# Expert tiles of 256 rows of one expert become tiles of two 128-row halves with an expert each

## What is computed

```
def _ffn(xf, w1, b1, w2, b2):
    h = jnp.maximum(xf @ w1 + b1, 0.0)
    return h @ w2 + b2
logits = x_flat @ router_w + expert_bias
top_vals, top_idx = jax.lax.top_k(logits, TOP_K)          # TOP_K = 2, 16 experts
weights = jax.nn.softmax(top_vals, axis=-1)
...
for e in range(N_EXPERTS):
    y_e = _ffn(x_flat, routed_w1[e], routed_b1[e], routed_w2[e], routed_b2[e])
    routed_out = routed_out + comb[:, e:e + 1] * y_e       # comb is 0 for experts not chosen
return shared_out + routed_out
```

## Time and profile before

| | |
|---|---|
| time, median of 3 runs | 887.23 us (885.23 to 887.95) |
| span of the profiled execution | 888.7 us |
| TensorE (PE) busy | 794.8 us, 89% |
| VectorE (DVE) busy | 471.0 us, 53% |
| ScalarE (ACT) busy | 483.6 us, 54% |
| GpSimd (POOL) busy | 552.2 us, 62% |
| mean DMA rate | 71 GB/s |

### The profile page before, as it was taken

The page is one execution under the profiler, slowest core; times in us unless marked ns, Lnnn a source line. Parts: engine busy times, 40 slices in busy tenths (PEclk is TensorE's granted clock), DMA queues, the critical chain, the costliest instruction groups (busy, mean ns, idle before and its releaser), DMA issues.

```text
span 888.7 us, 24132 instructions
## 1 busy us (share of the span) xinstructions
PE 794.8 (89%) x8070; PEld 572.5 (64%) x8071; DVE 471.0 (53%) x1381; ACT 483.6 (54%) x1147; POOL 552.2 (62%) x691
## 2 busy tenths in 40 slices
PE   4788999999999999999977679999999999999791
PEld 1344556655566565655554359999999999988440
DVE  2436787677767877678754423333333333332076
ACT  2355666566556666565644316666666665655147
POOL 5445588787878888787876624555555555445344
PEclk9988999999999999999999879999999999999997
DMA  5001021220222112220115321222222222221394
GB/s 165 13 27 27 19 61 56 68 62 25 61 58 65 46 40 62 62 62 29 48 32 186 124 71 46 70 70 67 71 65 65 65 65 61 65 64 46 109 317 142
DMA packets 70324, 63.44 MB, mean 71 GB/s; under 512 B 8002, under 2 KB 61640, under 8 KB 70112
## 3 DMA queue, kind: packets, MB, share of 16 engines
q1 hardware_dynamic: 60816, 44.99, 18.0%
q0 software_dynamic: 9152, 17.07, 5.9%
q10 hardware_dynamic: 272, 0.26, 0.1%
HBM read 38.75 MB, written 25.50 MB: 72 GB/s over the span
## 4 chain that ended last, share of the span: by engine, by line
PE 72%; issue 7%; POOL 6%; DVE 6%; ACT 3%; another core or an unknown queue 2%; DMA 2%; DVEq 0%; SPq 0%; POOLq 0%; ACTq 0%
PE psO L616 16%; PE psB L605 15%; PE psO L541 7%; PE psP L332 5%; PE psB L485 4%; POOL w_ring L945 3%; PE psO L548 3%; PE psB L443 3%; PE psP L407 2%; PE psP L323 2%; PE psB L475 2%; PE psP L596 2%; PE psP L347 2%; PE psB L463 2%
## 5 line engine op out<-in xcount | busy, mean ns | idle before, releaser
L988 POOL DMA_INDIRECT expert_results<-yw_all,rows x158 | 155.3, 983 | 160.0 <-ACT yw_all L863 131.2
L616 PEld LDWEIGHTS psO<-w_sb,hide 128*128 128x128 f32 x1264 | 152.9, 192 | 6.6 <-issue 2.9
L616 PE MATMUL psO<-w_sb,hide 128*128 x1264 | 154.6, 275 | 0.6 <-ACT hide L855 0.5
L965 POOL DMA_INDIRECT dispatched_rows<-rows,slot x128 | 131.0, 1023 | 36.7 <-issue 32.6
L855 ACT ACTIVATE hide<-psB,w_ring 128x256 f32<-128x256 f32 x316 | 123.6, 474 | 54.6 <-PE psB L605 50.8
L605 PE MATMUL psB<-x1T,w_ring 128*128 128x256 f32 x632 | 149.9, 380 | 0.7 <-DVE x1T L1289 0.4
L1302 DVE TENSOR_TENSOR K<-psO,b_sb 128x256 f32<-128x256 f32 x79 | 33.6, 425 | 173.0 <-PE psO L616 141.8
L605 PEld LDWEIGHTS psB<-x1T,w_ring 128*128 128x128 f32 x632 | 113.9, 190 | 13.9 <-issue 1.7
L945 POOL TENSOR_TENSOR w_ring<-w_ring,tot 128x128 f32<-128x128 f32 (+2 forms) x160 | 117.9, 758 | 0.0
L863 ACT ACTIVATE yw_all<-K,rows 128x128 f32<-128x128 f32 x158 | 54.8, 394 | 79.3 <-issue 48.4
L1040 DVE SCALAR_TENSOR_TENSOR psP<-psP,cols,delta 128x512 f32<-128x512 f32 x80 | 57.4, 754 | 71.7 <-PE psP L332 71.7
(11 more groups left out here) (174 smaller groups left out, 1311.5 us busy)
## 6 DMA issues: line engine op xcount, KB each, us to landing
rows<-dispatched_rows SPq DMA_DIRECT2D x80, 132.0 KB
w_sb<-expert_results SPq DMA_DIRECT2D x8, 1024.0 KB, 11.9
h_res<-in_hidden SPq DMA_DIRECT2D x16, 256.0 KB
out<-w_sb SPq DMA_DIRECT2D x16, 256.0 KB, 2.3
hT<-in_hidden_t SPq DMA_DIRECT2D x15, 256.0 KB, 4.6
w_sb<-in_w SPq DMA_DIRECT2D x14, 256.0 KB
expert_results<-yw_all,rows POOLq DMA_INDIRECT x158
dispatched_rows<-pad_rows SPq DMA_DIRECT2D x17, 132.0 KB
```

Of the source, the lines that this page charges most:

```text
L616: last = mm(psO[:, p, s * 128:(s + 1) * 128], hide[p][:, c, s * 128:(s + 1) * 128], w2_sb[:, bass.ds(e, 1), c, :].rearrange("p e c -> p (e ...
L965: G.indirect_dma_start(rows_dram[:, :], bass.IndirectOffsetOnAxis(slot[u % 2][:, j, k:k + 1], 0), rows[k][u % 2][:, j, :], None).then_inc( ...
L988: G.indirect_dma_start(back_dram[:, :], bass.IndirectOffsetOnAxis(row_in[i][:, s, AT_DEST:AT_DEST + 1].bitcast(u32), 0), yw[i][:, s, :], N ...
```

## The change

A tile is still 256 rows, but now two halves of 128 (`PART`), and the table gives each half its own expert and its own first row. Counts are rounded up to 128: (16384 + 16 x 127) / 128, rounded down, is 143 halves, so 72 tiles in place of 79. The buffers of rows and results go from 8 to 6 (`RING`), those of w1 from 4 tiles to 3 (`W_RING`), each now of two copies. `load_rows` issues one DMA of 128 rows for each half, four for a pair of tiles. `e_up` makes eight products of 128 columns in place of four of 256, half by half. `e_w1` copies w1 twice and also copies b2 of both experts into a new buffer, `b2b`. A new VectorE operation, `e_hid2`, does the two half-tile activations of hidden block 2; ScalarE does the other six, and waits for VectorE's before block 3. TensorE reads two registers per tile in `e_down`. VectorE's loop is now `e_y(j)`, `e_xT(j + 3)`, `e_w1(j + 3)`, `e_hid2(j + 2)`. `make_table` makes twice as many entries, and the pads are half as long.

```diff
 ST = 256
 SUB = ST // 128
-RING = 8
-W_RING = 4
-ETILES = (N * TOPK + EXPERTS * (ST - 1)) // ST
-TABLE = -(-ETILES // RING) * RING
-CAP = N + ST
+RING = 6
+W_RING = 3
+PART = 128
+ETILES = -(-((N * TOPK + EXPERTS * (PART - 1)) // PART) // SUB)
+TABLE = -(-ETILES // RING) * RING * SUB
+CAP = N + PART
...
+        w1b = [[w1_ring[:, 2 * i + s, :] for s in range(SUB)] for i in range(2)]
+        w1b.append([t[:, 0:HIDDEN + HC] for t in (o_sq[:, :, :].rearrange("p n v -> p (n v)"), R_near[:, :, :, :].rearrange("p c h t -> p (c h t)"))])
+        b2b = [mixed[i // 2][:, i % 2, :].rearrange("p (s c) -> p s c", c=C) for i in range(W_RING)]
...
-            def load_rows(j, i):
+            def load_rows(j, i, turn):
                 if not (isinstance(j, int) and j < RING):
-                    sp.wait_ge(sem(f"e_back{i // 2}"), (j - i) * (2 * SUB * 16 // RING))
+                    sp.wait_ge(sem(f"e_back{i // 2}"), turn * (2 * SUB * 16))
                 for t in range(2):
-                    sp.nop(nofuse=True)
-                    r = sp.value_load(tile_ri[0:1, bass.ds(j + t, 1)], min_val=0, max_val=EXPERTS * CAP)
-                    sp.dma_start(row_in[i + t], rows_dram[bass.ds(r, ST), :].rearrange("(s p) c -> p s c", p=128)).then_inc(sem(f"e_rows_in{i // 2}"), 16)
+                    for s in range(SUB):
+                        sp.nop(nofuse=True)
+                        r = sp.value_load(tile_ri[0:1, bass.ds(j * SUB + t * SUB + s, 1)], min_val=0, max_val=EXPERTS * CAP)
+                        sp.dma_start(row_in[i + t][:, s, :], rows_dram[bass.ds(r, PART), :]).then_inc(sem(f"e_rows_in{i // 2}"), 16)
             done(sp, "base_out", UNITS - 2)
             for j in range(0, RING, 2):
                 if j == RING - 2:
                     done(sp, "base_out", UNITS - 1)
-                load_rows(j, j)
-            with sp.Fori(0, TABLE // RING - 1) as ring:
+                load_rows(j, j, 0)
+            with sp.Fori(0, ETILES // RING - 1) as ring:
                 for i in range(0, RING, 2):
-                    load_rows(sp.snap(ring * RING + (i + RING)), i)
...
-            def e_turn(j, i):
-                pe.wait_ge(sem(f"e_rows_in{i // 2}"), (j - i) * (32 // RING) + 32)
+            def e_turn(i, turn):
+                pe.wait_ge(sem(f"e_rows_in{i // 2}"), turn * (2 * SUB * 16) + 2 * SUB * 16)
                 for s in range(SUB):
                     last = nc.tensor.transpose(psP[i % 2][:, s * 128:(s + 1) * 128], row_in[i][:, s, 0:C], mat("ident"))
                 last.then_inc(sem("e_turn_ps"))
 
-            def e_up(j, i):
+            def e_up(j, i, w):
                 p = i % 2
                 pe.wait_ge(sem("e_xT"), j + 1)
                 pe.wait_ge(sem("e_w1"), j + 1)
                 pe.nop(nofuse=True)
                 for c in range(HC):
-                    last = mm(up_ps(p)[:, c // 2, (c % 2) * ST:(c % 2 + 1) * ST], w1b[i % W_RING][:, c * 128:(c + 1) * 128], xTe[p],
-                              start=True, stop=True)
+                    for s in range(SUB):
+                        at = (c % 2) * ST + s * PART
+                        last = mm(up_ps(p)[:, c // 2, at:at + PART], w1b[w][s][:, c * 128:(c + 1) * 128], xTe[p][:, s * PART:(s + 1) * PART],
+                                  start=True, stop=True)
                 last.then_inc(sem("e_up_ps"))
 
             def e_down(j, i):
                 p = i % 2
-                e = pe.value_load(tile_ei[0:1, bass.ds(j, 1)], min_val=0, max_val=EXPERTS - 1)
+                es = [pe.value_load(tile_ei[0:1, bass.ds(j * SUB + s, 1)], min_val=0, max_val=EXPERTS - 1) for s in range(SUB)]
                 pe.wait_ge(sem("e_hid"), j + 1)
+                pe.wait_ge(sem("e_hid2"), j + 1)
                 pe.nop(nofuse=True)
                 for s in range(SUB):
                     for c in range(HC):
                         last = mm(psO[:, p, s * 128:(s + 1) * 128], hide[p][:, c, s * 128:(s + 1) * 128],
-                                  w2_sb[:, bass.ds(e, 1), c, :].rearrange("p e c -> p (e c)"), start=(c == 0), stop=(c == HC - 1))
+                                  w2_sb[:, bass.ds(es[s], 1), c, :].rearrange("p e c -> p (e c)"), start=(c == 0), stop=(c == HC - 1))
                 last.then_inc(sem("e_down_ps"))
...
             with pe.Fori(0, (ETILES - 1) // RING) as ring:
                 for i in range(RING):
-                    e_turn(pe.snap(ring * RING + (i + 2)), (i + 2) % RING)
-                    e_up(pe.snap(ring * RING + (i + 1)), (i + 1) % RING)
-                    e_down(pe.snap(ring * RING + i), i)
+                    e_turn((i + 2) % RING, pe.snap(ring + (i + 2) // RING))
+                    e_up(pe.snap(ring * RING + (i + 1)), (i + 1) % RING, (i + 1) % W_RING)
+                    e_down(pe.snap(ring * RING + i), i % RING)
...
-            def e_hid(j, i):
+            def e_hid(j, i, w):
                 p = i % 2
                 act.wait_ge(sem("e_up_ps"), j + 1)
-                for c in range(HC):
-                    last = A(hide[p][:, c, :], psB[:, 2 * p + c // 2, (c % 2) * ST:(c % 2 + 1) * ST], ACT.Relu,
-                             bias=w1b[i % W_RING][:, HIDDEN + c:HIDDEN + c + 1])
+                for c in (0, 1, 3):
+                    if c == 3:
+                        act.wait_ge(sem("e_hid2"), j + 1)
+                    for s in range(SUB):
+                        at = (c % 2) * ST + s * PART
+                        last = A(hide[p][:, c, s * PART:(s + 1) * PART], psB[:, 2 * p + c // 2, at:at + PART], ACT.Relu,
+                                 bias=w1b[w][s][:, HIDDEN + c:HIDDEN + c + 1])
                 last.then_inc(sem("e_hid"))
...
-            def e_w1(j, i):
-                e = dve.value_load(tile_ei[0:1, bass.ds(j, 1)], min_val=0, max_val=EXPERTS - 1)
+            def e_w1(j, w):
+                es = [dve.value_load(tile_ei[0:1, bass.ds(j * SUB + s, 1)], min_val=0, max_val=EXPERTS - 1) for s in range(SUB)]
                 if not (isinstance(j, int) and j < W_RING):
                     dve.wait_ge(sem("e_hid"), j + (1 - W_RING))
-                dve.nop(nofuse=True)
-                V.tensor_copy(w1b[i % W_RING][:, :], w1_sb[:, bass.ds(e, 1), :].rearrange("p e n -> p (e n)")).then_inc(sem("e_w1"))
-
-            def e_y(j, p):
-                e = dve.value_load(tile_ei[0:1, bass.ds(j, 1)], min_val=0, max_val=EXPERTS - 1)
+                    dve.wait_ge(sem("e_hid2"), j + (1 - W_RING))
+                    dve.wait_ge(sem("e_y"), j + (1 - W_RING))
+                dve.nop(nofuse=True)
+                for s in range(SUB):
+                    V.tensor_copy(b2b[w][:, s:s + 1, :], b2_sb[:, bass.ds(es[s], 1), :])
+                    last = V.tensor_copy(w1b[w][s], w1_sb[:, bass.ds(es[s], 1), :].rearrange("p e n -> p (e n)"))
+                last.then_inc(sem("e_w1"))
+
+            def e_hid2(j, p, w):
+                c = 2
+                dve.wait_ge(sem("e_up_ps"), j + 1)
+                for s in range(SUB):
+                    at = (c % 2) * ST + s * PART
+                    last = V.tensor_scalar(hide[p][:, c, s * PART:(s + 1) * PART], psB[:, 2 * p + c // 2, at:at + PART],
+                                           w1b[w][s][:, HIDDEN + c:HIDDEN + c + 1], 0.0, ALU.add, ALU.max)
+                last.then_inc(sem("e_hid2"))
+
+            def e_y(j, p, w):
                 dve.wait_ge(sem("e_down_ps"), j + 1)
-                dve.nop(nofuse=True)
-                V.tensor_tensor(ye[p], psO[:, p, 0:ST].rearrange("p (s c) -> p s c", c=C),
-                                b2_sb[:, bass.ds(e, 1), :].broadcast_to([128, SUB, C]), ALU.add).then_inc(sem("e_y"))
+                dve.wait_ge(sem("e_w1"), j + 1)
+                dve.nop(nofuse=True)
+                V.tensor_tensor(ye[p], psO[:, p, 0:ST].rearrange("p (s c) -> p s c", c=C), b2b[w], ALU.add).then_inc(sem("e_y"))
 
             dve.wait_ge(sem("w1_in"), 4 * 16)
-            for j in range(3):
+            for j in range(2):
                 e_w1(j, j)
-                if j < 2:
-                    e_xT(j, j)
-            with dve.Fori(0, (ETILES - 1) // W_RING) as quad:
-                for i in range(W_RING):
-                    dve.wait_ge(sem("e_up_ps"), quad * W_RING + (i + 1))
-                    e_xT(dve.snap(quad * W_RING + (i + 2)), i % 2)
-                    e_w1(dve.snap(quad * W_RING + (i + 3)), (i + 3) % W_RING)
-                    e_y(dve.snap(quad * W_RING + i), i % 2)
-            for j in range((ETILES - 1) // W_RING * W_RING, ETILES):
+                e_xT(j, j)
+            e_hid2(0, 0, 0)
+            e_xT(2, 0)
+            e_w1(2, 2)
+            e_hid2(1, 1, 1)
+            with dve.Fori(0, (ETILES - 3) // RING) as ring:
+                for i in range(RING):
+                    e_y(dve.snap(ring * RING + i), i % 2, i % W_RING)
+                    e_xT(dve.snap(ring * RING + (i + 3)), (i + 3) % 2)
+                    e_w1(dve.snap(ring * RING + (i + 3)), i % W_RING)
```

(38 more changed lines are left out.)

51 lines of the change are left out of this document (21 added, 30 removed).

## The result

The changed kernel took 985.17 us (median of 4 runs, 982.01 to 991.89) against 887.59 us for the kernel before beside it: a ratio of 1.113, 95% interval 1.109 to 1.117. It is 11% slower; 979 us was forecast. The profiled execution spans 984.1 us, 95.4 more than before.

A forecast was written before the change was run, and what follows sets the result against it. TensorE was taken to bound the kernel. Span: 888.7 - 21.5 (fewer tiles) + 82.5 (stalls) + 29 (clock) + 1.5 (edges) = 980.2 us, so a median of about 979 us; range 930 to 1012.

The forecast's parts named there:

- TensorE, -21.5 us: Expert stage: 72 iterations of 3.80 us in place of 79 of 3.735, if TensorE stays the bound: -21.5 us.
- The chain and the stall, +82.5 us: Row-buffer reuse: a 12.45 us chain against 7.6 us of cover stalls TensorE 4.85 us, 17 times: +82.5 us.
- The clock, +29 us: TensorE after each of 17 stalls: 3.4 us at half clock, 1.7 us lost each time: +29 us.
- the bounds of 0 and 41: Clock cost after stalls: 0 if the clock stays up, 41 us at 2.4 us per stall.
- VectorE, nothing: VectorE's longer iteration, 2.8 to 3.9 us against TensorE's 3.80, was charged nothing.
- The sum's upper end of 3.9 us: VectorE's operations in one iteration, added up: 3.9 us at most, against TensorE's 3.80.
- ready after 3.5 us and wanted after 4.0: VectorE's w1 copies for tile j + 3, both times counted from the end of tile j's second products.
- The rival that made VectorE the bound: Rows come in time and VectorE sets the pace at 4.3 us per iteration: 903 us, chance 0.04.
- The copy beside the scatter: GpSimd's scatters slowed by VectorE's w1 copies: 0.3 us each at the upper end; by the skill's rule, up to 0.43.
- The edges, +1.5 us: Outside the steady loop: three more VectorE table operations and delayed second and third tiles: +1.5 us.
- The rival without the clock: TensorE stalls for rows but its clock stays up: 950 us, chance 0.20.
- the two in which the rows come in time: Row loads never stall TensorE: 867 us, chance 0.05, or 903 us with VectorE as the bound, chance 0.04.

The follow-up runs named there:

- rows8_early: rows8 with VectorE's two register loads for tile j + 3 moved ahead of e_y(j): 836.33 us, 0.978 of the kernel before.
- before_rows6: The kernel before with six row and result buffers instead of eight, loops unrolled by twelve, w1 keeping four buffers: 952.86 us, ratio 1.083.
- rows8: The changed kernel with eight row and result buffers instead of six and four w1 buffers instead of three: 878.32 us, 0.997 of the kernel before.

## Why the prediction was right, point by point

**TensorE, -21.5 us: right.** The iterations between stalls take 3.79 us (649.77 to 653.56). From the first to the last start of the transposes lie 69 whole iterations and one short one ahead of them (2.8 us in the kernel before; I take the same): 264.3 us without stalls at full clock, an estimate, where the kernel before took 289.3. That is -25.0. rows8_early, which has no stall in the loop but a low clock in its first 4 us, took 266.5; its whole gain is 855.9 - 836.3 = 19.6.

**The chain and the stall, +82.5 us: right.** Measured +85.3, from 17 stalls as counted, 22.5 us apart and each followed by a pair without one; 5.02 us each for 4.85. Small errors cancel in part: the chain is 0.4 us longer than forecast, and the two iterations in front of it take 7.8 us up to the wait and not 7.6. Its steps:

| step | forecast | stall above | mean of the 17 |
|---|---|---|---|
| end of the products to the first issue | 6.77 (642.66 - 635.89) | 7.05 | 7.12 |
| three spacings | 1.38 + 2.5 = 3.9 | 3.56 | 3.78 |
| fourth issue to the rows | 1.8 | 2.09 | 1.91 |
| chain | 12.45 | 12.70 | 12.8 |

In the stall above the first step is longer since `e_y` starts 0.66 us behind the products and not 0.36; the mean over the stalls is 0.52. A load costs 1.26 us in the mean (1.19 above), the middle that I took the earlier trace rows. The landing came out by luck. I read 1.9 us for 132 KB at the end of the burst, where nobody waited; in before_rows6, where TensorE waits for such loads, 2.24 us pass at the median from the second issue to the transposes. With 66 KB it is 1.88 at the median, from the fourth issue. So half the size is worth 0.36 us, and some 0.3 us between the end of the burst and the start of the transposes, which I had left out, made up for it. My reason for taking off only 0.1, that most of the 1.9 is delay before the burst, was a misreading too: rows 6 show 0.7 us of delay and 1.1 of burst. The Trainium skill (DMA: Bandwidth & Descriptors, Anatomy of one DMA) gives a fixed cost of about 2.0 us to a DMA that GpSimd issues. These loads are SyncE's, so it need not hold for them, but the 1.9 to 2.2 us lie near it.

**The clock, +29 us: right in kind, too small.** This is the mis-sized term. The 17 iterations right behind a stall took 101.1 us together, where 17 x 3.79 is 64.4: 36.7 us lost, 2.2 per stall in place of 1.7. The step that was off is "3.4 us at half speed do 1.7 us of work": 11 of the 17 low stretches last 6.83 us and only 6 last 3.41. Here are an iteration with a short one and one with a long one (TensorE):

```profile
640.82 0.69 PE L602 MATMUL psP<-mats,rows 128*128 128x128 f32 x2 [4.64 <-DMA rows<-dispatched_rows]
641.30 3.05 PE L613 MATMUL psB<-x1T,w_ring 128*128 128x128 f32 x16
644.19 1.95 PE L625 MATMUL psO<-w_sb,hide 128*128 x16
645.97 0.38 PE L602 MATMUL psP<-mats,rows 128*128 128x128 f32 x2
...
662.47 0.69 PE L602 MATMUL psP<-mats,rows 128*128 128x128 f32 x2 [4.88 <-DMA rows<-dispatched_rows]
...
668.70 0.38 PE L602 MATMUL psP<-mats,rows 128*128 128x128 f32 x2
```

The first iteration takes 5.15 us, the other (662.47 to 668.70) 6.23, for 3.79: 1.36 and 2.44 us lost. In the mean it is 1.56 behind the 6 short stretches and 2.48 behind the 11 long ones, which makes up the 36.7. A part of each stretch lies in the stall itself, where it costs nothing. The clock costs about 37 us, inside the bounds of 0 and 41. A low clock in the first 6 us of the loop, ahead of all stalls of the ring, cost some 2.8 us more, which the forecast did not have.

**VectorE, nothing: right for this kernel, and wrong as a statement on VectorE.** Behind each stall it catches up, and TensorE's waits for it are 0.6 us at most in all. But the cover is gone once the stalls are: rows8 lost 19 us (72 x 0.26) to it. The sum's upper end of 3.9 us was near; what failed is "ready after 3.5 us and wanted after 4.0". The two were counted from different points: the 3.5 from the end of the products' record (634.11 + 1.95 = 636.06, and `e_y` 0.2 behind it), the 4.0 from the start of the transposes, 0.17 earlier; the margin was 0.3 us and not 0.5. The 1.49 us (0.89 and 0.6) from the start of `e_xT` to the first copy held: rows8 has 1.48 at the median, 2.07 at most. But `e_y` started 0.96 us behind the products at the median and not 0.36 as before, and those 0.6 us are more than the margin. Why `e_y` starts so late in rows8 stays open; with the register loads ahead of it, in rows8_early, it is 0.30. The rival that made VectorE the bound said 903 us for a case in which the rows come in time: in that case it came out at 0.997 of the kernel before, some 885 us on the chip of the result, with an iteration of 4.06 and not 4.3.

**The copy beside the scatter: smaller than either price.** In the changed kernel (ns, minimum, median, maximum):

```profile
L1001 POOL DMA_INDIRECT expert_results<-yw_all,rows x144: 980/983/1200, 536.2 to 930.9; - x144
...
L1316 DVE COPY w_ring<-w_sb x96: 415/422/700, 521.5 to 913.6; 128x516 f32 x96
```

The 66 scatters that overlap a w1 copy took 1.03 us in the mean and the 78 others 0.98: 0.05 us, not 0.3 and not 0.43. The longest took 0.22 more. The copy is held up as well, 0.46 beside a scatter for 0.42 alone, at worst 0.70. The rule of the Trainium skill (SBUF — State Buffer, SBUF: two separate sides) has its sign confirmed, since the two engines do slow each other. Its size is not: no scatter was held up for the length of a copy, and the mean price is about a tenth of the copy's duration. Over 17 stalls and 34 scatters that is 2 us, not 15.

**The edges, +1.5 us: wrong in sign.** The loop began 3.9 us earlier and what follows it took 4.2 us less, -8.1 in all. I did not look for the cause; runs of one kernel differ by some us.

**The sum.** -25.0 of work, +85.3 of waits, +36.7 of low clock behind the stalls, +2.8 of low clock at the loop's start, +3.7 in the stalled iterations beside the counted waits (most of it 0.16 us in each of the 17), -8.1 at the edges: 95.4 us; forecast +91.5. So the mechanism and the number of stalls were right, but that the total is off by only 4 us is partly luck: clock and stalls were forecast 17 us too small, the saved work 3.5 too small and the edges 9.6 too large. The rival without the clock fell (95.6 us of low stretches); so did the two in which the rows come in time.

## What to carry to other kernels

Where a profile shows no wait for a buffer, work out its slack: from the end of its last use to the landing of its new contents, against the iterations in between; and count again whenever the number of buffers or the number of DMAs behind one wait changes. Keep register loads ahead of a wait and not behind it, on a DMA queue as on a compute engine. A stall on TensorE costs more than its length when the clock falls after it, and an engine that looks covered has to be judged in the kernel without the stall.
